# Six states instead of two whose du times B comes from GpSimd, in a Mamba block with a mixture of experts on one Trainium2 core

## The reference, cut to what matters

```python
delta = softplus(dt @ dt_w.T + dt_b)              # [L, 256]
A = -exp(A_log)                                   # [256, 16]
def step(h, (u_t, d_t, B_t, C_t)):                # h: [256, 16]
    h = h * exp(d_t[:, None] * A) + (d_t * u_t)[:, None] * B_t[None, :]
    return h, einsum('ds,s->d', h, C_t)
y = scan(...) + xc * Dsk
y = (y * silu(z)) @ out_proj.T
```

## Time and profile before

| what | us |
|---|---|
| median of 3 runs (581.93, 582.24, 590.12) | 582.24 |
| the profiled execution | 584.82 |
| its span | 583.1 |
| first scan of unit 0, 1, 2, 3 starts at | 46.89, 156.16, 262.16, 374.88 |
| so units 0, 1, 2 take | 109.3, 106.0, 112.7 |
| busy: PE, DVE, ACT, POOL | 491.6, 450.5, 444.7, 342.7 |
| dBu transposes; scaled blocks on ScalarE | 992; 492 |

### The profile page before, as it was taken

How to read it: one execution, slowest core, us unless ns; L and a number is a source line. 1 busy time by engine, 2 the same in 40 slices (tenths; PEclk the granted TensorE clock), 3 DMA queues, 4 the chain that set the end, 5 groups by cost and what they waited for, 6 DMA issues and landing times.

```text
span 583.1 us, 9185 instructions
## 1 busy us (share of the span) xinstructions
PE 491.6 (84%) x3346; PEld 406.4 (70%) x3346; DVE 450.5 (77%) x689; ACT 444.7 (76%) x851; POOL 342.7 (59%) x167
## 2 busy tenths in 40 slices
PE   3586999969898999889989987888867487999996
PEld 2344966857786678777955777778856376698696
DVE  5887778849987786798887896778999998856322
ACT  2459788999988799999689999999769751473250
POOL 3103566877969788696887979756667672200000
PEclk9989899979999999999999997889979989968999
DMA  8031111312331322233222231222173114000101
GB/s 262 0 117 38 37 72 73 110 50 80 108 127 45 110 74 73 72 116 112 74 74 72 73 110 45 87 63 101 45 214 109 72 37 145 1 1 2 36 2 37
DMA packets 18237, 44.77 MB, mean 77 GB/s; under 512 B 1360, under 2 KB 7632, under 8 KB 17936
## 3 DMA queue, kind: packets, MB, share of 16 engines
q1 hardware_dynamic: 18192, 44.18, 22.6%
HBM read 42.61 MB, written 1.57 MB: 76 GB/s over the span
## 4 chain that ended last, share of the span: by engine, by line
PE 38%; ACT 36%; DVE 18%; issue 4%; POOL 2%; DMA 1%; POOLq 0%; DVEq 0%; ACTq 0%
ACT dBuT L661 16%; ACT dA L645 10%; PE pro L1314 10%; PE yT L1314 10%; DVE area L1101 9%; PE yT L1318 7%; PE dBu L1318 5%; PE dBu L1314 5%; ACT th L611 1%; DVE area L884 1%; PE pro L1318 1%; POOL hc L554 1%; ACT area L623 1%; ACT pre L620 1%; ACT area L635 1%
## 5 line engine op out<-in xcount | busy, mean ns | idle before, releaser
L554 POOL TENSOR_TENSOR hc<-area 128x1024 f32<-128x1024 f32 x127 | 300.2, 2368 | 129.0 <-DVE area L1098 68.3
L661 ACT ACTIVATE dBuT<-area,bT 128x256 f32<-128x256 f32 x492 | 208.6, 503 | 6.4 <-PE dBu L1318 6.4
L1318 PE MATMUL dBu<-ident,dBuT 128*128 128x128 f32 x992 | 141.0, 282 | 43.7 <-DVE area L1101 25.0
L1318 PEld LDWEIGHTS dBu<-ident,dBuT 128*128 128x128 f32 x992 | 114.7, 144 | 54.9 <-issue 22.3
L645 ACT ACTIVATE dA<-area,Aneg 128x1024 f32<-128x1024 f32 x124 | 141.9, 1147 | 12.7 <-DVE area L1101 12.6
L1318 PE MATMUL yT<-ident,hc 128*128 128x128 f32 x1024 | 139.6, 281 | 2.5 <-POOL hc L554 2.2
L1318 PEld LDWEIGHTS yT<-ident,hc 128*128 128x128 f32 x1024 | 120.1, 145 | 20.9 <-issue 15.2
L1098 DVE TENSOR_TENSOR_SCAN area<-dA,dBu 128x512 f32<-128x512 f32 x62 | 74.8, 1206 | 14.3 <-PE dBu L1318 11.6
L1098 DVE TENSOR_TENSOR_SCAN area<-dA,area,dBu 128x512 f32<-128x512 f32 x62 | 79.2, 1277 | 5.3 <-PE dBu L1318 1.5
L1101 DVE TENSOR_TENSOR_SCAN area<-dA,area,dBu 128x512 f32<-128x512 f32 x62 | 79.2, 1278 | 4.4
L1101 DVE TENSOR_TENSOR_SCAN area<-dA,dBu 128x512 f32<-128x512 f32 x62 | 74.6, 1204 | 8.6 <-PE dBu L1318 8.2
(11 more groups left out here) (240 smaller groups left out, 609.9 us busy)
## 6 DMA issues: line engine op xcount, KB each, us to landing
area<-bc_rows SPq DMA_DIRECT2D x64, 512.0 KB, 3.7
dBuT<-w_in SPq DMA_DIRECT2D x1, 2048.0 KB, 9.2
wp<-wpack_in SPq DMA_DIRECT2D x1, 1030.0 KB, 7.4
x<-x_in SPq DMA_DIRECT2D x2, 512.0 KB, 6.4
hc<-bcast_in SPq DMA_DIRECT2D x1, 1024.0 KB, 10.5
Bb<-bc_rows SPq DMA_DIRECT2D x2, 512.0 KB, 3.9
out<-x SPq DMA_DIRECT2D x4, 256.0 KB, 2.3
bc_rows<-xdbl SPq DMA_DIRECT2D x4, 128.0 KB, 3.8
```

The source lines that it names most:

```text
L554: g_.tensor_tensor(hc[:, e % 3, :], hs[:, e % 3, :], Cb[:, g % 3, :], ALU.mult).then_inc(hc_done, 1)
L661: return nc.scalar.activation(dBuT[:, SCALED.index(g) % 2, n, :], duT[par][:, n, :], ACT.Copy, scale=bT[:, par, n, s:s + 1])
L1318: return nc.tensor.matmul(out, in_, ident[:, :] if idn is None else idn, start=start, stop=True, is_transpose=True, skip_group_check=True)
```

## The change

DIRECT grows from two states to six, two in each of the units 0 to 2: states 4 and 11 in units 0 and 1, 4 and 13 in unit 2 (t = 8, 9; t = 22, 23; in unit 2 t = 26, 27). The second of each pair lies right behind softplus. Each product is made alone, after the hc of one tile (`PRODUCT_AFTER`: t = 1 and 3 for the first state; t = 8 and 10, in unit 2 t = 10 and 12, for the second), and is held until its scan in a buffer that is idle then (`hold`): the delta of the other parity, gz, or yg. softplus waits for the scans of the first state, two of the products for the items that last read their buffer. SP loads the row of B after Cb of states 0 and 6. ScalarE: for the first state of a unit the item comes between the two chunk exps and the scaled blocks behind them; for the second, both chunk exps of its first tile stand behind softplus, those of its second tile in the next two tiles, and exp of the tile behind it one tile early. In unit 1 nothing stands in t = 21 and 22, then Z0, Z1 (t = 23, 24), DU0 to DU3 (25 to 28), Z2, Z3 (29, 30). The gain and add instructions of the first norm move from t = 14, 16 to 15, 18.

```diff
--- before.py
+++ after.py
@@ -45,7 +45,7 @@
 
 
 NORM_AT = {9: 0, 10: 1, 24: 5, 25: 6}
-SCALE_AT, GAIN_AT, ADD_AT, LNX_AT = 12, 14, 16, 31
+SCALE_AT, GAIN_AT, ADD_AT, LNX_AT = 12, 15, 18, 31
 POW_AT = (10, 25)
 
 
@@ -79,7 +79,7 @@
             if u == 0:
                 items = early + [("Z", j, 0) for j in range(4)] + x + steps + [None, None] + z + turns
             elif u + 2 < NU:
-                items = early + turned + x + steps + added + z + turns
+                items = early + turned + x + steps + added + [None, None] + z[0:2] + turns + z[2:4]
             else:
                 items = early + turned + added + z[0:2] + x + steps + [None, None] + turns + z[2:4]
         at = NH * DS * u
@@ -107,7 +107,10 @@
 PARTS, ENDS, SP_AT = schedule()
 
 
-DIRECT = [DS * u + s for u, s in [(1, 4), (2, 4)]]
+DIRECT_AT = {(0, 4): (1, 3), (0, 11): (8, 10), (1, 4): (1, 3), (1, 11): (8, 10), (2, 4): (1, 3), (2, 13): (10, 12)}
+DIRECT = [DS * u + s for u, s in DIRECT_AT]
+PRODUCT_AFTER = {NH * DS * u + t: (k, half) for k, ((u, s), ts) in enumerate(DIRECT_AT.items()) for half, t in enumerate(ts)}
+FIRST_ROW, SECOND_ROW = 0, 6
 SCALED = [g for g in range(NG) if g not in DIRECT]
 ORDER = [(k, j, 0) for k, j in FIRST_ITEMS]
 ORDER += [it for it in ENDS if it is not None]
@@ -194,6 +197,16 @@
         yg = area3[:, 6:6 + NH, :]
         du = pre
         Bb = sb("Bb", [P, L])
+
+        def hold(g, half):
+
+            u, par = g // DS, g // DS % 2
+            if g == DIRECT[2 * u]:
+                return delta[1 - par][:, half, :]
+            if u == 1:
+                return gz[0].rearrange("p n d -> p (n d)")[:, half * L:(half + 1) * L]
+            return yg[:, half, :]
+
         wtap = sb("wtap", [P, 2, DC, DI])
         Aneg = sb("Aneg", [P, 2, NH, DS])
         dskip = sb("dskip", [P, 2, NH, P])
@@ -452,12 +465,13 @@
                     wait_item(sp, "LG", 0, 0)
                     for dst, lo, hi in ((w2a, 0, 4), (w2b, 4, 6), (w2c, 6, 8)):
                         sp.dma_start(dst, w2_d[lo:hi].rearrange("e (c p) h -> p e c h", p=P)).then_inc(s_w2, 16)
-                if g + 1 in DIRECT:
-                    k = DIRECT.index(g + 1)
+                sp.dma_start(Cb[:, g % 3, :], crow_d[u, DS + s:DS + s + 1, :].partition_broadcast(P)).then_inc(cb_ready[g % 3], 16)
+                if u + 1 < NU and s in (FIRST_ROW, SECOND_ROW):
+                    k = 2 * u + (s == SECOND_ROW)
+                    row = DIRECT[k] % DS
                     if k:
                         sp.wait_ge(direct_ready, NH * k)
-                    sp.dma_start(Bb[:, :], crow_d[u, s + 1:s + 2, :].partition_broadcast(P)).then_inc(bb_ready, 16)
-                sp.dma_start(Cb[:, g % 3, :], crow_d[u, DS + s:DS + s + 1, :].partition_broadcast(P)).then_inc(cb_ready[g % 3], 16)
+                    sp.dma_start(Bb[:, :], crow_d[u, row:row + 1, :].partition_broadcast(P)).then_inc(bb_ready, 16)
 
             sp.wait_ge(dbu_ready, dbu_count(NT - 1, NCH - 1))
             sp.dma_start(w1s, w1_d.rearrange("e h f -> h e f")).then_inc(s_w1, 16)
@@ -503,13 +517,16 @@
                 g_.tensor_tensor(du[:, half, :], delta[par][:, half, :], xc[par][:, half, :],
                                  ALU.mult).then_inc(du_ready, 1)
 
-            def direct_product(e):
-
-                k, half = DIRECT.index(e // NH), e % NH
+            def direct_product(k, half):
+
+                u = DIRECT[k] // DS
                 g_.wait_ge(bb_ready, 16 * (k + 1))
-                g_.wait_ge(du_ready, NH * (e // (DS * NH)) + half + 1)
-                g_.wait_ge(scan_done, NCH * (e - 2))
-                g_.tensor_tensor(dA[:, e % 3, :], du[:, half, :], Bb[:, :], ALU.mult).then_inc(direct_ready, 1)
+                g_.wait_ge(du_ready, NH * u + half + 1)
+                if k % 2 and u == 1:
+                    wait_item(g_, "YT", NH * NCH - 1, 0)
+                elif k % 2 and u == 2:
+                    wait_item(g_, "O", NCH - 1, 1)
+                g_.tensor_tensor(hold(DIRECT[k], half), du[:, half, :], Bb[:, :], ALU.mult).then_inc(direct_ready, 1)
 
             pows = [0]
 
@@ -544,14 +561,13 @@
                     pool_du(product_at(e), e // (DS * NH) + 1)
                 if e == NT - 1:
                     break
-                if e % NH == 0 and e // NH + 1 in DIRECT:
-                    direct_product(e + NH)
-                    direct_product(e + NH + 1)
                 g_.wait_ge(scan_done, NCH * (e + 1))
                 g_.wait_ge(cb_ready[g % 3], 16 * (g // 3 + 1))
                 if e >= 3:
                     g_.wait_ge(yacc_done, e - 2)
                 g_.tensor_tensor(hc[:, e % 3, :], hs[:, e % 3, :], Cb[:, g % 3, :], ALU.mult).then_inc(hc_done, 1)
+                if e in PRODUCT_AFTER:
+                    direct_product(*PRODUCT_AFTER[e])
                 t2 = e - NH * DS * (NU - 2)
                 if t2 in POW_AT:
                     rstd_pow(0)
@@ -631,6 +647,7 @@
             def softplus(u):
                 _, _, par = unit(u)
                 wait_item(act, "DT", NH * NCH - 1, u)
+                act.wait_ge(scan_done, NCH * NH * (DIRECT[2 * (u - 1)] + 1))
                 for half in range(NH):
                     nc.scalar.activation(delta[par][:, half, :], pre[:, half, :], ACT.Softplus).then_inc(delta_ready, 1)
 
@@ -713,12 +730,19 @@
             scale_blocks(1, 0)
             for e in range(NT):
                 g, half = divmod(e, NH)
-                direct = (e + 1) // NH in DIRECT
                 u, t = divmod(e, DS * NH)
+                direct = u + 1 < NU and (e + 1) // NH == DIRECT[2 * u]
                 since = t - SP_AT[u] if u + 1 < NU else -1
-                if direct:
+                if since in (1, 2):
+                    exp_chunk(NH * DS * u + SP_AT[u] + 4, since - 1)
+                elif since == 3:
+                    exp_tile(e + 2)
+                elif direct:
                     exp_chunk(e + 1, 0)
-                elif e + 1 < NT and since not in (1, 2):
+                    if e and ENDS[e - 1] is not None:
+                        item_a(*ENDS[e - 1])
+                    exp_chunk(e + 1, 1)
+                elif e + 1 < NT and since != 4:
                     exp_tile(e + 1)
                 if since == 0:
                     exp_tile(e + 2)
@@ -731,13 +755,12 @@
                         scale_blocks(g + 1, 1)
                     if g + 2 < NG and (g + 2) % DS != 0 and g + 2 not in DIRECT:
                         scale_blocks(g + 2, 0)
-                if direct:
-                    exp_chunk(e + 1, 1)
-                if e and ENDS[e - 1] is not None:
+                if e and not direct and ENDS[e - 1] is not None:
                     item_a(*ENDS[e - 1])
                 if since == 0:
                     softplus(u + 1)
-                    exp_tile(e + 3)
+                    for i in range(NCH):
+                        exp_chunk(e + 3, i)
                 if e == NH * DS * (NU - 2) + SCALE_AT:
                     first_norm(1, acc, acc).then_inc(first_scaled, 1)
                 elif e == NH * DS * (NU - 2) + LNX_AT:
@@ -1092,7 +1115,7 @@
                 lo, hi = c * CH, (c + 1) * CH
                 decay, inflow = dA[:, e % 3, lo:hi], dBu[q % 3][:, :]
                 if direct:
-                    decay, inflow = inflow, decay
+                    decay, inflow = inflow, hold(e // NH, e % NH)[:, lo:hi]
                 if u % 2 == 0:
                     init = hs[:, e % 3, lo - 1:lo] if i else 0.0
                     nc.vector.tensor_tensor_scan(hs[:, e % 3, lo:hi], decay, inflow, init, ALU.mult, ALU.add).then_inc(scan_done, 1)
```

## The result

| | before | after |
|---|---|---|
| median of 20 runs each, us | 584.19 (580.52 to 590.12) | 591.42 (585.60 to 594.79) |
| ratio of the times, 95% interval | | 1.0097 (1.0068 to 1.0125) |
| profiled execution, us; its span | 584.82; 583.1 | 588.77; 587.0 |

The kernel became 1% slower: the sign of the forecast's +1.9 us, but more of it, and the median lies 2.4 us above the range. The profiled execution grew by 3.95 us where the working had 1.9.

What follows compares the result with a forecast made beforehand. ScalarE and VectorE's scans were taken to set the pace by stage, with gains only in the stalls. Units 0, 1, 2 at -2.6, +2.0, +2.5 gave +1.9 us: 586.7 profiled, 584.1 on the median; range 577 to 589, own range 581 to 588.

Steps and rivals of the forecast that it cites:

- From profile to median: Last step: the counterpart of the profiled execution, 586.7 us, becomes 584.1 on the median of 582.24, 2.6 lower.
- Unit 0, state 11: Behind softplus in unit 0: ScalarE's queue to tanh of Z0 shortens from 15.9 to 14.1 us, -1.75.
- I take +0.25 (bounds 0 and 1): Same stall in unit 0: TensorE's longer idle gap, with its low clock after it, costs 0.25 us.
- Unit 0, state 4: Unit 0, tiles 5 to 8 and the X items: tanh runs earlier, -1.1 us (bounds 0 and -2.8).
- Unit 1: Sum of unit 1's terms: state 4's new order, state 11 and the moved Z items, +2.0 us.
- State 11 at -0.65: Unit 1 behind softplus: the wait for O0 shrinks, but chunk exps wait for scans; -0.65 us (bounds 0 and -2.8).
- Z at +3.7: End of unit 1: Z2 and Z3 behind the DU copies get their tanh late, +3.7 us (bounds 0 and 4.3).
- Unit 2: Sum of unit 2's terms: state 4 +0.5, pow behind product +2.3, softplus -0.3, together +2.5 us.
- the pow: Unit 2, state 13: its first product delays the first norm's pow by 2.36; +2.3 us (bounds 0 and 2.4).
- softplus: Unit 2 behind softplus: TensorE stands at DU1, then restarts; -0.3 us (bounds -0.9 and +0.8), +0.2 by the clock rule.
- rival c: Tiles 8 to 13, units 0 to 2: GpSimd falls over two tiles behind, delaying scans by up to 14.2: 596.4 us; chance 0.13.
- Rivals a and b: a: ScalarE's saved work turns into time, 569.9 us, chance 0.04; b: the two new waits don't bite, 578.1 us, chance 0.20.

Runs made afterwards that it cites:

- filled_after: The changed kernel plus turns of a zero block on TensorE behind softplus, 56, 16 and 56 in units 0, 1, 2: 586.47 us, ratio 1.0045.
- four_states_filled: The changed kernel with only state 4 of units 0 to 2 and unit 0's state 11 direct, Z early, 60 zero turns at tile 21: 582.67 us.
- z_order: The changed kernel with unit 1's Z items back ahead of the DU turns, state 11's product held in duT[0]: 587.35 us, ratio 1.0068.
- pow_first: The changed kernel with the first norm's pow ahead of the direct product on GpSimd in unit 2: 590.44 us, ratio 1.0113.
- filled_before: The kernel before plus zero turns on TensorE behind softplus, 36 in unit 0 and 28 in unit 2: 584.88 us, ratio 1.0021.
- all_mended: The changed kernel with unit 1's Z early, the pow ahead of the product, and 56 zero turns at tiles 21 and 89: 587.16 us, ratio 1.0033.
- products_twice: The changed kernel with each direct product made twice on GpSimd, 12 more products: 603.26 us, ratio 1.0346.
- first_states: The changed kernel with only state 4 of units 0 to 2 direct, softplus and unit 1's items as before: 583.81 us, ratio 0.9971.
- du_first_filled: The changed kernel, DU turns ahead of Z in units 0 and 1, pow first, zero turns at tiles 21, 22 and 89: 587.43 us, ratio 1.0041.

## Why the prediction was wrong

The queues and the sign of each unit were foretold rightly. Two steps failed: the one from the profile to the median, which put the result out of the range, and the price of the low clock in unit 0, which is the larger part of what the sum missed.

- *From profile to median, the step that failed for the range.* The working has 586.7 for the profiled execution and then, "on the median of 582.24, 2.6 lower, it is 584.1". The 2.6 came from three executions of the kernel before, which themselves spread from 581.9 to 590.1, and it was carried over to a kernel that had not run. Over 20 executions the median of before lies 0.6 under its profile and that of after 2.65 above its own. Of the miss of 7.3 us the sum has 2.05 and this step 5.2: 1.95 because the three executions were quick ones, and 3.3 because after lies higher against its profile. With the measured 3.95 in the sum and this step as it stood, the forecast would have been 586.2, inside the range. With the 3.3 goes a lower clock: 12 of the 20 executions of after have a mean clock of 0.933 or less, and of the kernel before none whose clock is at hand is under 0.939.
- *Unit 0, state 11, with the clock, the step that failed in the sum.* -1.75 for the queue was about right: with the clock held it is -2.1 (filled_after, four_states_filled). "I take +0.25 (bounds 0 and 1)" was not: the same code with the clock as it falls gives -0.3, a cost of 1.85 us, nearly twice the upper bound (0.97 in z_order, 1.98 in pow_first). I had priced a gap that is a little longer. What changed is the place: before, the slow matmuls lie inside VectorE's wait for tanh and cost nothing (filled_before); after, they stand behind it, and ScalarE waits for TensorE over three tiles.
- *Unit 0, state 4:* -1.1 expected, -0.37 measured (8 to 15, in every run that has it). Against tile 8, the first tanh of an X item came 0.7 earlier, not 1.3, the second 0.1, not 0.7; that is inside the bounds of 0 and -2.8. Unit 0's other 0.5 is the first eight tiles, which also vary by themselves. The sign that I named, tile 23 earlier by 2.6 to 2.9, came short with 2.42, and those 0.5 are in it.
- *Unit 1:* +2.0 expected, +2.36 measured, so the number is near, but in part by luck. State 4 is -0.89 (-1.05 expected). State 11 at -0.65 and Z at +3.7 don't exist as two prices: 0.33 and 2.93 in one order of adding them, 3.0 and 0.26 in the other, half of the 3.0 being clock. The waits of 1.0 and 1.7 us at the last tiles came as foretold.
- *Unit 2:* +2.5 expected, +2.45 measured; here too the parts miss more than their sum. State 4 is +0.8 (0.5), and +0.2 to +1.1 over the runs, as the clock holds or falls at tile 74; the pow +1.7 (2.3), softplus -0.16 (-0.3). The last is the place where a rule was weighed. The rows first: against before, tiles 88 to 96 are 1.05 us shorter with the clock held, 0.16 shorter in the changed kernel and 0.73 longer in pow_first, nearly the span from -0.9 to +0.8 that bounded the term. The Trainium skill, "TensorE: Matmul & The Clock Gate", What's actually happening, says that the default is throttled and activity lifts it; the runs agree: with 56 turns of zeros in the gaps of units 0 and 2 the granted clock stays at 1.00 in filled_after, though it fell behind the zeros of unit 0 in all_mended.
- *GpSimd (rival c):* no scan waited for hc beyond 0.3 us, so its queue had no part in the slowdown but by the pow in unit 2. products_twice shows the point from which it would, one more product in the same gap.
- *Rivals a and b:* both fell. ScalarE's saved work became idle time, and both new waits bit, with 2.7 and 1.7 us.

What stays open: where the changed kernel's slower executions lose their time. No profile of after caught one. pow_first gives a hint: it differs from after by the order of two pieces of GpSimd's work, all its six executions have a mean clock of 0.927 or 0.928, and its profile has the untouched stretch behind unit 3 at 104.88 us, 6.1 more. The four executions of after at 0.928 lie some 6 us above its slowest at 0.939 (594.4 to 594.8 against 588.8). That fits the same loss, and doesn't show it. Nor is it known why z_order, whose tiles 8 to 96 take 303.44 in its profile, has a median of 587.35.

## What to carry to other kernels

Work taken off an engine that is full on the average pays only where the queue behind it is full at that place: look at what the shorter instruction waits for next (here a bank that the scan frees), and at which consumer stands behind it. Two changes that use the same slack have no separate prices; measure them in a square of four, and see that the clock was the same in all fields. Look where TensorE's slow stretch lies: inside another engine's wait it cost nothing here, behind that wait up to 2 us. Some turns of zeros can show this and, where no real work has to stand behind them, mend it. And a median is not a profile plus a constant: take the spread of whole executions into the range.

## What the runs showed of the hardware

**The clock's luck is as large as the effect.** The stretch from the end of unit 3 to the end of the span is the same code in all 14 kernels profiled. It took 98.6 to 98.8 us in seven profiles, 104.8 or 104.9 in five, 100.4 and 101.7 in two. The table by stage of first_states, where it took 104.80, and of after, where it took 98.76; first the whole stretch, then the same 20 us of each, counted from the stretch's start:

```profile
481.55:586.35 104.80, 94.31 (x609) 83.28 (x609) 53.47 (x180) 36.15 (x104) 3.30 (x2) 0.85 0.08 28
513.30:533.30 20.00, 20.00 (x96) 19.31 (x96) 12.50 (x49) 8.54 (x34) 0.00 (x0) 0.50 0.00 1
```

```profile
488.29:587.05 98.76, 88.12 (x609) 77.35 (x609) 53.56 (x179) 36.15 (x104) 3.31 (x2) 0.91 0.09 29
520.00:540.00 20.00, 18.72 (x126) 17.92 (x126) 13.95 (x56) 9.92 (x38) 0.00 (x0) 0.76 0.01 1
```

The 609 matmuls are the same; in first_states they stay at the low clock longer, and TensorE is busy 6.2 us more. Unit 3, whose code no kernel touches either, took from 107.7 (filled_before) to 111.8 us (du_first_filled), at a mean clock of 0.94 and 0.91. So a gain of 2 us upstream vanishes or triples in one whole time, and it is why this study reads stages; and a stage is only safe where the clock was the same. The Trainium skill, "TensorE: Matmul & The Clock Gate", What's actually happening, holds the ramp's penalty to be under 1% of a typical kernel's span; it speaks of the first ramp. Here the low level returns, and a single untouched stretch differs by 6.1 of 585 us, 1.05%, between profiles.

**Idle GpSimd is not free GpSimd.** It is idle 39% of the changed kernel's span, yet of the 28.3 us (12 x 2.36) that a second product in each gap adds, 14.6 come out in the time.
